# Cross-attention and a routed expert layer: each expert's first 128 rows get a block of their own

## The reference

```python
expert_id = jnp.argmax(scores, axis=-1)
h = gelu(jnp.einsum('bsh,ehf->ebsf', x, w1) + b1[:, None, None, :])
y = jnp.einsum('ebsf,efh->ebsh', h, w2) + b2[:, None, None, :]
out = jnp.einsum('ebsh,bse->bsh', y, jax.nn.one_hot(expert_id, 8))
```

## Time and profile before

| | us |
|---|---|
| median of 3 runs (lowest, highest) | 234.27 (232.66, 235.13) |
| the profiled execution's own time | 234.39 |
| its span, first to last instruction | 232.7 |
| TensorE busy (share of the span) | 201.1 (86%) |
| VectorE busy | 180.6 (78%) |
| ScalarE busy | 157.9 (68%) |
| GpSimd busy | 128.6 (55%) |

### The profile page before, as it was taken

The page is one execution under the profiler, slowest core; times in us unless marked ns, Lnnn a source line. Parts: engine busy times, 40 slices in busy tenths (PEclk is TensorE's granted clock), DMA queues, the critical chain, the costliest instruction groups (busy, mean ns, idle before and its releaser), DMA issues.

```text
span 232.7 us, 5011 instructions
## 1 busy us (share of the span) xinstructions
PE 201.1 (86%) x1837; PEld 150.3 (65%) x1837; DVE 180.6 (78%) x395; ACT 157.9 (68%) x249; POOL 128.6 (55%) x177
## 2 busy tenths in 40 slices
PE   0379969999999999989989899899993797999980
PEld 0133417776766767757666566789973686899970
DVE  2899797697998998998995997958756435776872
ACT  2752899399399699699595799689531445667650
POOL 3695718807915807978508947744400740066763
PEclk9999985899999999999999999999996569999998
DMA  6999979899999999999999999988994369999200
GB/s 215 389 251 263 226 223 237 192 234 174 220 215 216 278 230 269 241 198 233 216 213 256 184 220 258 201 196 185 239 263 121 120 219 290 346 370 378 98 11 12
DMA packets 142958, 51.78 MB, mean 223 GB/s; under 512 B 121172, under 2 KB 140773, under 8 KB 142934
## 3 DMA queue, kind: packets, MB, share of 16 engines
q1 hardware_dynamic: 142000, 50.08, 93.2%
q0 software_dynamic: 784, 1.38, 1.7%
q10 hardware_dynamic: 150, 0.00, 0.0%
HBM read 10.74 MB, written 3.75 MB: 62 GB/s over the span
## 4 chain that ended last, share of the span: by engine, by line
PE 49%; DVE 21%; DMA 11%; issue 8%; ACT 4%; POOL 3%; SPq 2%; DVEq 0%; POOLq 0%
DMA PT<-Phl 10%; PE psX L1079 5%; PE psS L1061 5%; PE psO L1079 5%; PE psS L1060 5%; PE psS L1059 5%; DVE S L800 5%; DVE Phl L817 3%; PE psS L1290 3%; PE psX L1081 3%; PE psO L1081 3%; ACT S L651 3%; SPq L393 2%; PE psS L1276 2%; PE psS L1296 2%
## 5 line engine op out<-in xcount | busy, mean ns | idle before, releaser
L651 ACT ACTIVATE S<-S,negb 128x1024 f32<-128x1024 f32 x48 | 55.1, 1147 | 18.4 <-DVE negb L808 18.4
L800 DVE TENSOR_SCALAR_CACHE_REDUCE S<-psS 128x1024 f32<-128x1024 f32 x48 | 58.2, 1217 | 11.4 <-PE psS L1061 11.2
L817 DVE TENSOR_TENSOR Phl<-S,Phl 128x1024 f16<-128x1024 f32 x38 | 51.5, 1355 | 5.0 <-ACT Phl L666 4.8
L533 POOL TENSOR_TENSOR Phl<-S,Phl 128x256 f16<-128x256 f32 x40 | 26.3, 689 | 51.7 <-ACT Phl L666 51.7
L666 ACT CAST Phl<-S 128x1024 f16<-128x1024 f32 x48 | 50.3, 1047 | 5.2 <-DMA PT<-Phl 3.7
L1059 PE MATMUL psS<-qT,gh 128*128 128x512 f16 x96 | 37.7, 393 | 5.4 <-DVE S L800 2.6
L1079 PE MATMUL psX<-qn,PT 128*128 128x256 f16 x204 | 36.4, 273 | 2.1 <-DMA PT<-Phl 2.1
L1079 PE MATMUL psO<-qn,PT 128*128 128x256 f16 x204 | 37.3, 276 | 0.9 <-DMA PT<-Phl 0.8
L1061 PE MATMUL psS<-qT,gl 128*128 128x512 f16 x96 | 37.9, 395 | 0.0
L1060 PE MATMUL psS<-qT,gh 128*128 128x512 f16 x96 | 37.9, 394 | 0.0
L1081 PE MATMUL psO<-qn,PT 128*128 128x128 f16 x204 | 35.7, 221 | 0.0
(11 more groups left out here) (239 smaller groups left out, 425.3 us busy)
## 6 DMA issues: line engine op xcount, KB each, us to landing
PT<-wp SPq DMA_DIRECT2D x8, 512.0 KB, 6.0
stageT<-in_ctxT SPq DMA_DIRECT2D x6, 512.0 KB, 7.0
qn<-wp SPq DMA_DIRECT2D x6, 512.0 KB, 7.3
wp<-in_w SPq DMA_DIRECT2D x4, 512.0 KB, 4.9
stageT<-in_w SPq DMA_DIRECT2D x4, 512.0 KB, 4.9
rows_by_expert<-stageT SPq DMA_DIRECT2D x4, 385.5 KB, 5.6
PT<-Phl SPq DMA_TRANSPOSE x48, 4.2
S<-rows_by_expert SPq DMA_DIRECT2D x2, 258.0 KB, 5.4
```

Of the source, the lines that this page charges most:

```text
L533: last = nc.gpsimd.tensor_tensor(lo[:, r], slot(t, e)[:, r], hi[:, r], ALU.subtract)
L651: nc.scalar.activation(slot(t, e), slot(t, e), ACT.Exp, bias=negb[:, t:t + 1], accum_out=Lp[:, t * NG + e:t * NG + e + 1]).then_inc(exp_do ...
L800: nc.vector.tensor_scalar(out=into, in0=bank(u, n)[:, 0:into.shape[1]], scalar1=1.0 / GS, scalar2=None, op0=ALU.mult, op1=ALU.max, accum_o ...
L817: nc.vector.tensor_tensor(lo, slot(t, e), hi, ALU.subtract).then_inc(low_done, 1)
```

## The change

The first 128 rows of expert e now always go to block e, for each of the eight experts, whether it has that many or not. Only rows beyond 128 go to further blocks; there can be at most NX = 6 of them, blocks 8 to 13. There are 14 sent blocks as before. Blocks 0 to 7 read their weights and bias selectors in place (`wp`, `pick`); only the six further blocks have a weight copy, and each has a slot of its own. All copies now stand behind the reads of the first two batches. The position of a row is its rank plus 128 times its expert, plus a shift if the rank is 128 or more. The dense blocks stand at turns 0 to 4, 10, 20 and 21.

```diff
-    NB = TA + E - 1
+    NX = TA - 1
+    NB = E + NX
-    DENSE_AT = (0, 1, 2, 3, 4, 10, 16, 21)
+    DENSE_AT = (0, 1, 2, 3, 4, 10, 20, 21)
-    ROUTE_CONSTS = 19
-    WSLOTS = 12
-    FIRST = 2
+    ROUTE_CONSTS = 21
...
-            sp.reg_load(expert_reg[0:FIRST], bexp[0:1, 0:FIRST])
-            ex = [sp.snap(r, min_val=0, max_val=E - 1) for r in expert_reg[0:FIRST]]
-            def fetch(b):
-                if b >= WSLOTS:
-                    sp.wait_ge(y_in_psum, SENT_AT[b - WSLOTS] + 1)
-                sp.dma_start(block_w(b), wp[:, :, bass.ds(ex[b] * F, F)]).then_inc(block_w_landed[b % WSLOTS], 16)
+            sp.reg_load(expert_reg[0:NX], bexp[0:1, 0:NX])
+            ex = [sp.snap(r, min_val=0, max_val=E - 1) for r in expert_reg]
+            def fetch(k):
+                sp.dma_start(block_w(k), wp[:, :, bass.ds(ex[k] * F, F)]).then_inc(block_w_landed[k], 16)
...
-            for b in range(FIRST):
-                fetch(b)
-            sp.reg_load(expert_reg[FIRST:NB], bexp[0:1, FIRST:NB])
-            ex += [sp.snap(r, min_val=0, max_val=E - 1) for r in expert_reg[FIRST:NB]]
             sp.wait_ge(rows_sent, 16 * TA)
             block_rows(0, 0, D, rows_landed)
             block_rows(1, 0, D, rows_landed)
+            block_rows(0, D, ROW, rest_landed)
+            block_rows(1, D, ROW, rest_landed)
+            block_rows(2, 0, D, rows_landed)
+            fetch(0)
+            block_rows(2, D, ROW, rest_landed)
+            fetch(1)
+            block_rows(3, 0, D, rows_landed)
             fetch(2)
...
             block_rows(3, D, ROW, rest_landed)
-            for b in range(10, NB):
-                fetch(b)
+            for k in range(3, NX):
+                fetch(k)
...
+            numbers(tri[:, :, E], E, [[-P, E]], base=(E - 1) * P)
...
             statistics(x1, TA, T)
+            link(nc.vector.tensor_copy(extra[:, E:E + 1], ones[:, 0:1]))
             dve.wait_ge(ranks_in_psum, 1)
...
-            link(nc.vector.tensor_tensor(rank[:, :, :], rank_psum.rearrange("p (t e) -> p t e", e=E),
-                                         sblk[:, :].unsqueeze(1).broadcast_to([P, TA, E]), ALU.add))
+            link(nc.vector.scalar_tensor_tensor(out=over[:, :, :], in0=ranks, scalar=float(P),
+                                                in1=shift[:, :].unsqueeze(1).broadcast_to([P, TA, E]),
+                                                op0=ALU.is_ge, op1=ALU.mult))
+            link(nc.vector.scalar_tensor_tensor(out=rank[:, :, :], in0=iob.broadcast_to([P, TA, E]), scalar=float(P),
+                                                in1=ranks, op0=ALU.mult, op1=ALU.add))
+            link(nc.vector.tensor_tensor(rank[:, :, :], rank[:, :, :], over[:, :, :], ALU.add))
             link(nc.vector.tensor_tensor(rank[:, :, :], rank[:, :, :], oneh[:, :, :], ALU.mult))
...
-                if b in SENT_AT:
-                    return block_w(SENT_AT.index(b))
-                k = DENSE_AT.index(b)
-                return wp[:, :, k * F:(k + 1) * F]
+                j = SENT_AT.index(b) if b in SENT_AT else DENSE_AT.index(b)
+                return wp[:, :, j * F:(j + 1) * F] if j < E else block_w(j - E)
...
-                    pe.wait_ge(block_w_landed[j % WSLOTS], 16 * (j // WSLOTS + 1))
-                    pe.wait_ge(chosen_rows, 1)
+                    if j >= E:
+                        pe.wait_ge(block_w_landed[j - E], 16)
+                        pe.wait_ge(chosen_rows, 1)
```

More of the change, by code:

```diff
@@ L87, in sem @@
             return es.enter_context(nc.semaphore(name))
-        tri = sb("tri", [P, E, E])
+        tri = sb("tri", [P, E, E + 1])
         mv = sb("mv", [P, T, 2])
@@ L141, in build @@
         iota_e = sb("iota_e", [P, E])
-        kedge = sb("kedge", [P, E, TA])
-        slot_no = sb("slot_no", [P, NB, E])
+        kedge = sb("kedge", [P, E, NX])
+        slot_no = sb("slot_no", [P, NX, E])
         row_no = sb("row_no", [P, 1])
@@ L150, in build @@
         empty = stageT[:, E * F + E * P // 2:E * F + E * P // 2 + ROW]
-        ints = stageT[:, XRE - NB * E:XRE].bitcast(I32)
+        ints = stageT[:, XRE - NX * E:XRE].bitcast(I32)
         w1raw = w2p[:, :, :].rearrange("p a n -> p (a n)").bitcast(F32)
@@ L166, in build @@
         rows = carve(NB * ROW).rearrange("p (b w) -> p b w", w=ROW)
-        more = carve(E * TA).rearrange("p (a b) -> p a b", b=TA)
-        below = carve(E * E).rearrange("p (a b) -> p a b", b=E)
+        more = carve(E * NX).rearrange("p (a b) -> p a b", b=NX)
+        below = carve(E * (E + 1)).rearrange("p (a b) -> p a b", b=E + 1)
         rank = carve(TA * E).rearrange("p (a b) -> p a b", b=E)
+        over = carve(TA * E).rearrange("p (a b) -> p a b", b=E)
         cand = carve(T * E).rearrange("p (a b) -> p a b", b=E)
         mask = carve(E)
-        chosen = carve(NB // 2, F16)
-        past = carve(NB * E).rearrange("p (a b) -> p a b", b=E)
+        chosen = carve(NX // 2, F16)
+        past = carve(NX * E).rearrange("p (a b) -> p a b", b=E)
         oneh = carve(TA * E // 2, F16).rearrange("p (a b) -> p a b", b=E)
-        nblk, sblk, eblk = carve(E), carve(E), carve(E)
-        posf, rmx, bexpf = carve(TA), carve(T), carve(NB)
-        pos, bexp = carve(TA, I32), carve(NB, I32)
+        extra, shift, eblk = carve(E + 1), carve(E), carve(E)
+        posf, rmx, bexpf = carve(TA), carve(T), carve(NX)
+        pos, bexp = carve(TA, I32), carve(NX, I32)
         parts_ring = Phl[:, :, :, :].rearrange("p r a w -> p (r a w)")
@@ L272, in build @@
         rest_landed = [sem(f"rest_landed{g}") for g in range(len(BATCHES))]
-        block_w_landed = [sem(f"block_w_landed{k}") for k in range(WSLOTS)]
+        block_w_landed = [sem(f"block_w_landed{k}") for k in range(NX)]
         chosen_rows = sem("chosen_rows")
@@ L359, in piece, with block_w @@
                     PT[:, 2 * e * TW:2 * e * TW + 2 * n, :])
[L361 to L365, removed]
+        def block_w(k):
+            half = (NX + 1) // 2
+            return spare[k // half][:, k % half * 4 * F:(k % half + 1) * 4 * F].rearrange("p (a f) -> p a f", f=F)
         @block.sync
@@ L432, in _ @@
                              empty[:, :].unsqueeze(1).broadcast_to([P, k1 - k0, ROW])).then_inc(slots_emptied, 16)
-            expert_reg = [sp.alloc_register(f"expert{j}") for j in range(NB)]
+            expert_reg = [sp.alloc_register(f"expert{j}") for j in range(NX)]
             sp.wait_ge(w_low, T)
             sp.wait_ge(experts_ready, 1)
-            sp.reg_load(expert_reg[0:FIRST], bexp[0:1, 0:FIRST])
-            ex = [sp.snap(r, min_val=0, max_val=E - 1) for r in expert_reg[0:FIRST]]
-            def fetch(b):
-                if b >= WSLOTS:
-                    sp.wait_ge(y_in_psum, SENT_AT[b - WSLOTS] + 1)
-                sp.dma_start(block_w(b), wp[:, :, bass.ds(ex[b] * F, F)]).then_inc(block_w_landed[b % WSLOTS], 16)
+            sp.reg_load(expert_reg[0:NX], bexp[0:1, 0:NX])
+            ex = [sp.snap(r, min_val=0, max_val=E - 1) for r in expert_reg]
+            def fetch(k):
+                sp.dma_start(block_w(k), wp[:, :, bass.ds(ex[k] * F, F)]).then_inc(block_w_landed[k], 16)
             def block_rows(g, a, b, done):
@@ L458, in _ @@
             block_rows(1, 0, D, rows_landed)
-            fetch(2)
[L460 to L471, removed]
+            block_rows(0, D, ROW, rest_landed)
[5 more added lines that the diff above has]
+            block_rows(3, 0, D, rows_landed)
+            fetch(2)
             block_rows(3, D, ROW, rest_landed)
-            for b in range(10, NB):
-                fetch(b)
+            for k in range(3, NX):
+                fetch(k)
             sp.wait_ge(y_ready, DENSE_AT[E - 1] + 1)
@@ L514, in _ @@
             numbers(iota_e[:, :], E, [[1, E]])
[L515 to L518, removed]
+            numbers(kedge[:, :, :].rearrange("p e k -> p (e k)"), E * NX, [[0, E], [P, NX]], base=P)
+            numbers(slot_no[:, :, :].rearrange("p b e -> p (b e)"), NX * E, [[P, NX], [-P, E]], base=(E - 1) * P)
+            then(nc.gpsimd.memset(tri[:, :, 0:E], float(P)))
+            then(nc.gpsimd.affine_select(out=tri[:, :, 0:E], in_=tri[:, :, 0:E], compare_op=ALU.is_gt, fill=0.0, base=0,
                                          pattern=[[1, E], [-1, E]], channel_multiplier=0))
+            numbers(tri[:, :, E], E, [[-P, E]], base=(E - 1) * P)
             then(nc.gpsimd.memset(ones16[:, :], 1.0))
@@ L944, in _ @@
             statistics(x1, TA, T)
+            link(nc.vector.tensor_copy(extra[:, E:E + 1], ones[:, 0:1]))
             dve.wait_ge(ranks_in_psum, 1)
-            link(nc.vector.tensor_tensor(more[:, :, :], count_psum.unsqueeze(2).broadcast_to([P, E, TA]),
+            link(nc.vector.tensor_tensor(more[:, :, :], count_psum.unsqueeze(2).broadcast_to([P, E, NX]),
                                          kedge[:, :, :], ALU.is_gt))
-            link(nc.vector.tensor_reduce(out=nblk[:, :], in_=more[:, :, :], axis=AX.X, op=ALU.add))
```

(25 more changed lines are left out.)

## The result

The changed kernel takes 250.2 us (median of 4 runs, 249.88 to 250.73) against 234.63 us for the kernel before: a ratio of 1.069, 95% interval 1.063 to 1.075. The forecast was 233.5, in a range of 231.7 to 235.4. The profiled execution took 250.35 us, its span is 248.6.

The account below looks back on a forecast made before the run. The prediction took GpSimd's last scatter and drain to bound the end, with TensorE setting the pace before it. From 234.39 us, +0.70 - 0.2 - 1.38 = -0.88 gave 233.5 us, range 231.7 to 235.4.

Parts of the forecast that it names:

- The step that failed: Whole kernel: the change touches only the part after about 177 us, so no term was given to the attention before it.
- all three: Rivals in the expert part: TensorE's clock returns later (0.20), the end does not move (0.15), quieter DMA gives more (0.17).
- The longer chain, +0.70: VectorE's position chain between L947 and L957: one added copy (0.20) and two full steps (0.25 each) delay everything behind.
- The last scatter, -1.38: At the end: sent blocks finish with number 19, so GpSimd's last indirect store and its drain come 1.38 us earlier.
- rival 2: At the end: GpSimd's drain waits for the dense store or block 21, losing the -1.38: 234.9 us; chance 0.15.
- The early copies, -0.2, by way of one slow scatter: Rows' way out and back: without two early copies one scatter loses 0.37 us, saving 0.2 us, bounds 0 and -0.5.
- Copies do not slow the products, blocks stay 1.61 us apart: Expert products on TensorE: nothing waits for weight copies, so dropping eight of fourteen directly gives 0; spacing stays 1.61 us.
- The clock: TensorE in the expert part: full clock returns 0.7 us later with the work; if fixed in time, 233.2 us.
- rival 1: TensorE in the expert part: a clock return later by t costs t/2, 235.3 us at t = 3.5; chance 0.20.
- The sum without the shift, -0.88: Whole kernel: the forecast's total of +0.70, -0.2 and -1.38 us, giving 233.5 us.

Follow-up runs that it names:

- tri last: The changed kernel with the declaration of `tri` moved from first to last tensor, instructions and their order unchanged: 232.53 us, 0.991 of the kernel before.
- two steps fewer: Against tri last, GpSimd writes the column of ones and the expert's offset is added in the position chain's last step: 231.76 us, 0.992 of the kernel before.
- with 16: Against tri last, dense blocks put back at turns 16 and 21 instead of 20 and 21: 233.03 us, 0.995 of the kernel before.
- the wider tri: The kernel before with `tri` one unused column wider, so all tensors behind it start 32 bytes later: 251.91 us, 1.073 of the kernel before.
- the target moved: Against tri last, only `PT`, which the attention's transposes write, starts 32 bytes past a multiple of 256: 233.08 us, 0.992 of the kernel before.
- the two early copies: Against tri last, two of the six weight copies put back ahead of the rows: 236.55 us, 0.997 of the kernel before.

## Why the prediction was wrong

**The step that failed** is the first: "The change touches only the part after about 177 us, so every term below lies there." I read the diff for its instructions and left out its declarations. The term was put at nothing and measured 17.7 us (232.5 with tri last, 250.2 as changed), 17.0 of them before the last transpose starts (166.5 and 183.5 us). No rival had that in it: all three began behind 177 us. The trace could not show the price, since every large tensor stood on a multiple of 256. It did show the exposure: the transposes were 10% of the chain of waits, and the page of before has DMA at 9 tenths in nearly every slice of the attention:

```profile
DMA  6999979899999999999999999988994369999200
```

The Trainium skill (DMA: Bandwidth & Descriptors, How a descriptor splits into AXI transactions) says that a descriptor is read in pieces, each of which must start at a multiple of 256 bytes. By that rule, an estimate, 256 bytes that start elsewhere are read in two pieces instead of one. The runs agree in that the boundary is 256 and that the source pays (1.056 against 0.992); no trace shows the pieces themselves. That page of the Trainium skill also counts the bytes fetched ahead of the start as beats of 32 bytes; by that count, an estimate for 256 bytes, 32, 64 and 128 bytes of shift would cost 9, 10 and 12 beats against 8, and so grow. No growth is measured (250.2, 248.7 and 248.9 us).

**The other terms**, with the large one taken out by tri last:

- *The longer chain, +0.70*: right. The first expert product comes 5.64 us after the chain's start instead of 4.95, +0.69, and two steps fewer give 0.44 back.
- *The last scatter, -1.38*: right in mechanism, about 1.0 in size. By itself the edit gave -1.2 us (-0.4 to -2.1), and the drain moved ahead of the dense store. From the first expert product to the drain's start it is 47.0 to 47.4 us in the seven profiles that have the dense blocks at 20 and in which the clock, once back, stays up (47.1 with tri last: 181.66 to 228.8), against 48.2 before and 48.1 with 16 (50.2 with the wider tri, in which TensorE waited 2.4 us for the rows). GpSimd's drain takes 1790 ns in each version, so rival 2 is out.
- *The early copies, -0.2, by way of one slow scatter*: the reading of the earlier trace rows was wrong. The fifth scatter takes 1.34 us with no copy beside it, in GpSimd's timeline of the changed kernel and then, with the seventh, with tri last:

```profile
202.59 1.34 POOL L591 DMA_INDIRECT rows_by_expert<-qT,S  x1 [0.30 <-issue]
```

```profile
184.87 1.34 POOL L591 DMA_INDIRECT rows_by_expert<-qT,S  x1 [0.30 <-issue]
187.77 0.96 POOL L591 DMA_INDIRECT rows_by_expert<-qT,S  x1 [0.30 <-issue]
```

  The read of the rows goes out 14.28 us after the chain's start with tri last; 13.67 before plus 0.69 would be 14.36. The relief is 0.1 us, not 0.4, and between single profiles 0.1 us is nothing.
- *Copies do not slow the products, blocks stay 1.61 us apart*: right, and no wait for a weight copy stands in the changed kernel's list of waits.
- *The clock*: the page's row after has its low slices again where the expert part begins, and no more of them:

```profile
PEclk9999999999999999999999999999998559999997
```

  Its return is fixed neither to the work nor to the time. In the changed kernel it lies at 204.8 us, 5.4 us after the first expert product instead of 7.2 before; with tri last it lies at 190.1, 8.4 us after it, and with the dense blocks back at 16 at 186.3, 5.5 us after it (all worked out like the 189.6 of the prediction). The changed kernel, then tri last:

```profile
204.00:205.00 1.00, 1.00 (x14) 1.00 (x12) 0.00 (x0) 0.95 (x2) 0.76 (x1) 0.61 0.37 132
190.00:191.00 1.00, 1.00 (x17) 0.95 (x15) 0.94 (x3) 1.00 (x3) 0.00 (x0) 0.97 0.00 0
```

  The price of rival 1, half of the delay, is not borne out by these two: the returns are 3.0 us apart, yet it is 47.2 and 47.1 us from the first product to the drain. In the changed kernel TensorE then waited 0.36 us for the rows; with tri last it did not. Two profiles in which the clock fell a second time, which no rival had, took longer: 49.0 us with the target moved and 51.0 with the two early copies; the waits for the rows, 0.6 and 2.1 us, are part of that.

The sum without the shift, -0.88, is smaller than what tri last gained (0.991, interval 0.987 to 0.995, thus -1.2 to -3.0 us). From the chain's start to the end of the span the profiles give 54.8 us with tri last and 55.3 before, only -0.5. The rest would lie ahead of the chain. The chain starts at 177.4 us before and at 176.0 with tri last, and the same attention brings it to 174.6 with the target moved, so single profiles cannot tell; what it is stays open.

## What to carry to other kernels

Read a diff's declarations as well as its instructions: a tensor that grows moves all that are placed behind it, and a stage that the edit does not touch can pay. Put small tensors of odd size behind the large ones, or pad them, and when a whole stage slows down in a trace although none of its lines changed, compare addresses before looking for a cause in the code. Start what a DMA transpose reads at a multiple of 256 bytes. A term of a few tenths of a microsecond is not read from one profile against another: hold the same stretch against as many profiles as there are.

## What the runs showed of the hardware that was not expected

- A DMA transpose that reads from 32, 64 or 128 bytes past a multiple of 256 takes 4.9 to 5.1 us to land instead of 4.1 to 4.2, and in a stage full of DMA this is 15 us of 137; a target shifted by 32 costs nothing (4.2 us).
- Of seven equal indirect scatters in a row the first takes 1.21 us, the fifth 1.32 to 1.34 and the others 0.96, in all twelve profiles, with or without weight copies beside them.
- TensorE's granted clock came back to full 5.4 us after the first expert product in one kernel's profile and 8.4 us after it in another's with the same instructions (it was 0.61 and 0.97 of full speed on average in the microsecond of the return).
